# Two halves' filter products issued together, in alternating row groups of TensorE

## The reference

```
emb = radial_embedding(edge_length)              # [E, 8]
h   = silu(emb @ mlp_w0 + mlp_b0)                # [E, 64]
h   = silu(h @ mlp_w1 + mlp_b1)                  # [E, 64]
w   = (h @ mlp_w2 + mlp_b2).reshape(E, 4, 32)    # the filter of an edge
ss, vv = xs[senders], xv[senders]                # gathered rows of a node table
m0 = w[:, 0] * ss
m1 = w[:, 1] * ss * Y1                           # Y1: direction of the edge
m2 = w[:, 2] * vv
m3 = w[:, 3] * (vv . Y1)
msg = segment_sum([m0, m3, m1, m2], receivers)   # [N, 256], then a small product and layer norm
```

## Time and profile before

| | |
|---|---|
| timed runs | 2207.32, 2209.00, 2209.87 us |
| profiled execution | 2202.79 us, span 2201.0 us |
| PE busy | 1899.1 us, 86% of the span |
| PE weight loads | 1431.4 us, 65% |
| DVE busy | 1370.4 us, 62% |
| ACT busy | 637.9 us, 29% |
| POOL busy | 1569.6 us, 71% |
| layer 0 gathers | from 44 to 1048 us |
| layer 1 gathers | from 1133 to 2150 us |
| finish | from 2158 us to the end |

### The profile page before, as it was taken

How to read it: one execution, slowest core, us unless ns; L and a number is a source line. 1 busy time by engine, 2 the same in 40 slices (tenths; PEclk the granted TensorE clock), 3 DMA queues, 4 the chain that set the end, 5 groups by cost and what they waited for, 6 DMA issues and landing times.

```text
span 2201.0 us, 34359 instructions
## 1 busy us (share of the span) xinstructions
PE 1899.1 (86%) x10138; PEld 1431.4 (65%) x10138; DVE 1370.4 (62%) x2905; ACT 637.9 (29%) x995; POOL 1569.6 (71%) x1599
## 2 busy tenths in 40 slices
PE   5887877778777887777879999999999999899997
PEld 4665666666666666666557777666776676677766
DVE  6755555555555555555645776666667666666665
ACT  3643343343433433432541111111111111111114
POOL 4777777777777777777147777777777777777770
PEclk8777777777777777777867998898999998988889
DMA  7422222222222222222021111111121221111112
GB/s 217 126 78 78 76 81 76 76 81 76 76 81 76 80 76 76 81 76 62 6 82 51 55 54 53 53 54 54 53 55 54 54 55 54 52 55 54 53 52 66
DMA packets 105683, 152.31 MB, mean 69 GB/s; under 512 B 33982, under 2 KB 65490, under 8 KB 105546
## 3 DMA queue, kind: packets, MB, share of 16 engines
q0 software_dynamic: 50656, 103.11, 17.3%
q1 hardware_dynamic: 54652, 46.76, 7.0%
q10 hardware_dynamic: 336, 2.01, 0.3%
HBM read 138.53 MB, written 13.21 MB: 69 GB/s over the span
## 4 chain that ended last, share of the span: by engine, by line
POOL 68%; issue 22%; PE 7%; DMA 1%; DVE 1%; ACT 1%; SPq 0%; POOLq 0%; DVEq 0%; ACTq 0%
POOL sent L436 68%; DMA unit_in<-in_x 1%; PE bank L984 1%; PE bank L800 1%; PE bank L767 1%; PE bank L815 1%; PE bank L953 1%; PE bank L759 1%; PE bank L988 0%; PE bank L942 0%; PE bank L871 0%; PE bank L879 0%; PE bank L802 0%; DMA sent<-up_table,senders 0%; DMA sent<-h_table,senders 0%
## 5 line engine op out<-in xcount | busy, mean ns | idle before, releaser
L436 POOL DMA_INDIRECT sent<-up_table,senders x784 | 775.3, 989 | 268.2 <-issue 237.7
L436 POOL DMA_INDIRECT sent<-h_table,senders x784 | 766.5, 978 | 263.9 <-issue 238.6
L815 PE MATMUL bank<-onehot,msg 128*128 128x128 f32 x4704 | 794.0, 332 | 7.1 <-DVE sums L1098 4.2
L815 PEld LDWEIGHTS bank<-onehot,msg 128*128 128x128 f32 x4704 | 706.4, 235 | 116.0 <-issue 91.4
L800 PE MATMUL bank<-Wf_sb,hid 128*128 128x128 f32 x1568 | 281.1, 334 | 94.8 <-DVE hid L1114 94.5
L1124 DVE TENSOR_TENSOR msg<-bank,sent 128x512 f32<-128x512 f32 x196 | 135.6, 692 | 349.1 <-issue 189.7
L800 PEld LDWEIGHTS bank<-Wf_sb,hid 128*128 128x128 f32 x1568 | 246.0, 239 | 153.5 <-DVE hid L1114 100.2
L800 PEld LDWEIGHTS bank<-w_sb,h 64*128 64x128 f32 x1568 | 195.5, 193 | 213.1 <-issue 116.2
L631 ACT ACTIVATE soft<-soft 128x512 f32<-128x512 f32 (+1 forms) x209 | 131.2, 628 | 591.2 <-DVE soft L1105 558.4
L1085 DVE TENSOR_TENSOR onehot<-relT,iota 128x512 f32<-128x512 f32 x392 | 268.8, 686 | 39.3 <-PE bank L815 37.1
L800 PE MATMUL bank<-w_sb,h 64*128 64x128 f32 x1568 | 233.9, 291 | 47.3 <-DVE msg L1157 46.4
(11 more groups left out here) (133 smaller groups left out, 1330.4 us busy)
## 6 DMA issues: line engine op xcount, KB each, us to landing
basis<-in_edge_weight SPq DMA_DIRECT2D x196, 100.0 KB
sent<-h_table,senders POOLq DMA_INDIRECT x784
sent<-up_table,senders POOLq DMA_INDIRECT x784, 2.5
basis<-near_lengths SPq DMA_DIRECT2D x196, 16.0 KB
radial_embedding<-basis SPq DMA_DIRECT2D x196, 16.0 KB
emb_in<-radial_embedding SPq DMA_DIRECT2D x98, 32.0 KB
unit_in<-in_x SPq DMA_DIRECT2D x12, 256.0 KB, 3.7
h_table<-h SPq DMA_DIRECT2D x12, 256.0 KB, 2.8
```

What stands on the lines that cost most here:

```text
L436: pool.indirect_dma_start(sent[:, n % SLOTS, j, :], None, table, bass.IndirectOffsetOnAxis(pick, 0))\
L815: last = t_.matmul(ps[:, k, :], msg[:, p, j, k * P:(k + 1) * P], onehot[:, p, j, :], start=(j == 0), stop=(j == HALF_CHUNKS - 1))
```

## The change

Layer 1's filters get four banks (2, 3, 6, 7: one per slot) in place of two. `filter1` now does both halves of a pair at once: for each of the four chunks it issues the product of the first half (rows 0 to 63 of `h2` and `w2_sb`) and then that of the second (rows 64 to 127), each into its own half's bank, and then the two bias products. So that the second half's bias product also lies in rows from 64 on, `ones_bf` and `bias3` get a second copy of their three rows at row 64, which takes three more small DMAs on SP. `filter1` is called at odd steps only, with the pair h-3 and h-2, where it was called at each step with half h-3. It waits for the messages of half h-6 (four halves before the pair's second) in place of half h-5.

```diff
-    ones_bf = sb("ones_bf", [3, P], BF16)
+    ones_bf = sb("ones_bf", [HIDDEN + 3, P], BF16)
...
-    bias3 = sb("bias3", [3, 3, P], BF16)
+    bias3 = sb("bias3", [HIDDEN + 3, 3, P], BF16)
...
+    filt1 = [quads[i] for i in (2, 3, 6, 7)]
...
         for part in range(3):
-            sp.dma_start(bias3[part:part + 1, :, :], bparts[:, part, :])\
-                .then_inc(d_bparts, 16)
+            for first in (0, HIDDEN):
+                sp.dma_start(bias3[first + part:first + part + 1, :, :], bparts[:, part, :])\
+                    .then_inc(d_bparts, 16)
...
         def filter1(h):
-            p, g = h.parity, h.pair_slot
-            b = h.before(2)
+            o = after(h, 1)
+            g = h.pair_slot
+            b = o.before(SLOTS)
             wait(pe, L1["msg"], b.upto())
             wait(pe, L1["act2"], h.pair_upto())
-            rows = slice(p * HIDDEN, (p + 1) * HIDDEN)
-            products(filtB[p], HALF_CHUNKS, P, lambda j: h2[rows, g, j * P:(j + 1) * P],
-                     w2_sb[rows, :], 2).then_inc(L1["filt"], 1)
+            for j in range(HALF_CHUNKS):
+                for q in (h, o):
+                    rows = slice(q.parity * HIDDEN, (q.parity + 1) * HIDDEN)
+                    t_.matmul(filt1[q.slot][:, j, :], h2[rows, g, j * P:(j + 1) * P],
+                              w2_sb[rows, :], start=(j == 0), stop=False, skip_group_check=True)
+            for q in (h, o):
+                three = slice(q.parity * HIDDEN, q.parity * HIDDEN + 3)
+                t_.matmul(filt1[q.slot], ones_bf[three, :],
+                          bias3[three, 2:3, :].broadcast_to([3, HALF_CHUNKS, P]),
+                          start=False, stop=True, skip_group_check=True).then_inc(L1["filt"], 1)
...
             b = h.before(3)
-            if b.real():
+            if b.parity == 0 and b.real():
                 filter1(b)
...
-        pe.wait_ge(d_bparts, 48)
+        pe.wait_ge(d_bparts, 96)
...
-            filt = filtB[p].rearrange("p j (i m) -> p j i m", m=MUL)
+            filt = filt1[h.slot].rearrange("p j (i m) -> p j i m", m=MUL)
```

More of the change, by code:

```diff
@@ L801, in products @@
                           skip_group_check=True)
-            return t_.matmul(out_bank[0:rows, 0:n_tiles, :], ones_bf[:, 0:rows],
-                             bias3[:, which:which + 1, :].broadcast_to([3, n_tiles, P]),
+            return t_.matmul(out_bank[0:rows, 0:n_tiles, :], ones_bf[0:3, 0:rows],
+                             bias3[0:3, which:which + 1, :].broadcast_to([3, n_tiles, P]),
                              start=False, stop=True, skip_group_check=True)
@@ L923, in layer1_any @@
                 second1(h)
-            filter1(h)
+                filter1(h)
             every_window(L1, every[1], h, 2)
```

## The result

The changed kernel takes 2210.9 us (median of 20 runs, 2206.2 to 2216.3), the kernel before on the same chip 2207.2 (20 runs, 2198.3 to 2212.7). The ratio is 1.0023, with a 95% interval of 1.0014 to 1.0032: slower by about 0.2%, or 3.7 us between the medians, where 7.5 were forecast. The profiled execution took 2212.1 us with a span of 2210.3, against 2202.8 and 2201.0 before: 9.3 us.

A forecast was written before the change was run, and what follows sets the result against it. Layer 1 was taken to be bound by POOL's gathers and the pauses between them. The terms -2 (stall), +5.5 (waits), +4 (end) and 0 (DMAs) made +7.5 on 2209.0: 2216.5 us, 8-in-10 range 2201 to 2226.

The forecast's parts named there:

- What bounds the kernel: Layer 1: POOL's gathers and the pauses between them set the time; PE is off the path except for 4 us.
- The Trainium skill's inference: Layer 1's gathers: by the skill comparisons hold none back, term 0, 2211 us; given 2 in 100 within the no-change case.
- PE's work: Layer 1's filter products: a pair takes 1.52 us instead of 3.10, none of the saving on the path.
- The stall at the start: Start of layer 1: POOL's 3.5 us standstill shrinks as messages come earlier; gain 1 to 3.5 us, taken as 2.
- The wait that goes: Layer 1: DVE's 47.2 us of waits for PE before `add_window` mostly go, moving its comparison; +5.5 us, bounds -7.8 and +11.0.
- the first pattern: Layer 1 iterations where DVE waits for rows only and two comparisons fall on gathers' starts: 20.93 us each, mean 20.69.
- The end: Last window and `finish`: PE at half clock costs +1.7 for the window and +2.6 for one block; taken as +4.
- SP's DMAs: Start of layer 0: three more small DMAs push back its first loads; bounds 0 and 2.5 us, taken as 0.
- The sum: Whole kernel: -2 + 5.5 + 4 + 0 = +7.5 us, on the profiled execution and the timed runs alike.
- it shortens the gathers: Rival, layer 1: small waits for PE settle in the second pattern, 20.52 us an iteration; 2203 us, chance 0.20.
- PE never became the bound: Rival, layer 1: PE stays at half clock over several pairs, each then costing 4 us; 2250 us, chance 0.03.
- Nothing comes of it: Rival, whole kernel: patterns mix as before, the stall's gain and the end's loss nearly cancel; +2, 2211 us, chance 0.27.

The follow-up runs named there:

- the last two kernels with the numbers in PSUM: The changed kernel with layer 1's comparison reading its column numbers from PSUM, 2169.7 us; the same with layer 0's comparison made of four scalar instructions, 2144.8 us.
- two paddings: The changed kernel with one DVE instruction added in layer 1 that nobody reads: a product of 0.28 us, 2193.0 us; or a small sum, 2204.9 us.

## Why the prediction was right, and where not

*What bounds the kernel* held. POOL waits for no message at all in the kernel after, the gathers' length sets the layer, and moving one operand of a comparison is worth 31 us in the kernel before, where four banks without the pairing of PE's products cost as much as the whole change.

*The Trainium skill's inference* ("SBUF — State Buffer", Who interferes with whom), that a product of two SBUF tensors doesn't hold up the writing of descriptors, doesn't carry over to these gathers. In the traces 95 of 95 were held with both operands in SBUF, none of 57 with one in PSUM, nor of the 41 and 48 in the last two kernels with the numbers in PSUM. The same section of the Trainium skill says that a DVE instruction with at most one SBUF input, outside its modes with two ports, doesn't contend with GpSimd; these counts agree. That the gather reads its list of senders in SBUF, and is held by the section's rule for instructions that read there, is argued and was not tried: no run here tells apart which part of a gather is held. The prediction's statement that the term would be nothing by the Trainium skill goes by the inference alone.

*PE's work*: 1.16 us for 16 products and 0.39 for the two biases, 1.13 and 0.39 as taken. Off the path, as said.

*The stall at the start*: forecast -2, measured -3.5: POOL waits for no message any more. The size is within the bounds, the reason only in part the one given. A pair's filters took 2.08 us at half clock, as taken, but for the first pair alone; then the clock was at its upper level, in a stretch where it had been at the lower one. The kernel before and the kernel after (columns as in the earlier trace rows), and PE in the kernel after:

```profile
1147.00:1168.00 21.00, 21.00 (x66) 14.04 (x65) 8.83 (x22) 2.06 (x3) 15.94 (x17) 0.50 0.20 57
```

```profile
1147.00:1184.00 37.00, 32.33 (x238) 22.57 (x236) 29.06 (x69) 6.88 (x10) 28.77 (x28) 1.00 0.20 55
```

```profile
1142.05 2.08 PE L881 MATMUL bank<-h,w_sb 128*128 128x512 f32 x2 [0.78 <-ACT h L696]
1144.05 2.08 PE L893 MATMUL bank<-w_sb,h 64*128 64x128 f32 x16
1146.07 0.58 PE L897 MATMUL bank<-bias,ones_bf 3*128 3x512 bf16 x2
```

The prediction had no term for a clock that rises some 20 us sooner, and why it did isn't shown. That the term came out is thus partly luck. POOL's wait is also gone in the kernel without the alternation, and not in the one with the banks alone; so it goes with both halves in one call, and the overlap isn't needed for it.

*The wait that goes*: forecast +5.5, half of the iterations in the first pattern; measured 45.2 - 34.4 = +10.8, that is nearly all of them, close to the upper bound of +11.0. What was mis-sized is the term against it, that PE falls behind by some 4 us in stretches at half clock. Its prices held: 2.08 us for a pair's filters, 2.08 for a dense product and 0.58 for the biases in the rows above, 3.79 for a window below. But the clock did not stay low for a pair. Between 1147 and 2158 us no 10.4 us, the time of two halves' gathers, has a granted clock under 0.67, that of this stretch:

```profile
1607.00:1617.40 10.40, 9.42 (x53) 7.45 (x54) 7.33 (x18) 0.69 (x1) 7.96 (x9) 0.67 0.22 60
```

PE is busy 9.4 of the 10.4 us there and isn't late, where the prediction had 14.4 us of work. Its window that ran at half clock, in the timelines of PE and DVE:

```profile
1607.98 3.79 PE L817 MATMUL bank<-onehot,msg 128*128 128x128 f32 x16 [1.88 <-DVE msg L1167]
1611.56 1.91 PE L881 MATMUL bank<-h,w_sb 128*128 128x512 f32 x2
1613.40 1.49 PE L893 MATMUL bank<-w_sb,h 64*128 64x128 f32 x16
1614.82 0.39 PE L897 MATMUL bank<-bias,ones_bf 3*128 3x512 bf16 x2
```

```profile
1607.84 0.41 DVE L1108 TENSOR_TENSOR sums<-sums,bank 128x256 f32 x1
...
1612.83 0.41 DVE L1108 TENSOR_TENSOR sums<-sums,bank 128x256 f32 x1
```

That window ended at 1611.77, a microsecond before DVE's next `add_window`, which started without a wait for PE, and PE came back to full clock in the course of the 16 products (1.49 us for 1.16; the biases take 0.39 again). DVE was not delayed, and so the pattern was not lost.

*The end*: forecast +4, measured +1.9 against the first profile. The last window at half clock came (+1.74); the block of `finish` at half clock did not, its products of L998 took 1.02 us from the first on. And the first profile was a lucky one here: against the other two of the kernel before, whose last window ran partly at half clock, the whole end is -0.8 and +0.2 us. So no cost of the change at the end is shown.

*SP's DMAs*: nothing of them is left at layer 1's start (first gather at 1133.02, before at 1132.98).

*The sum*: 7.3 for the gathers and their pauses and 1.9 for the end make the profiled pair's 9.3, against 7.5 forecast; against the two other profiles of the kernel before it is 9.9 and 6.7. The terms came out on both sides of the forecast (-1.5, +5.3 and -2.1 us off), so the nearness of their sum is partly luck. Between the medians it is 3.7, by the step "the sum holds for them alike", which is not shown to hold. The higher executions of the kernel before may have more iterations in the first pattern already, so that less is left to add; its three profiles, all below the median, don't show it, and this stays open. The measured 2210.9 us is thus below the forecast's own range of 2212 to 2224. Of the 5.6 us to 2216.5, 3.8 come from the difference and 1.8 from the median that it was added to, 2209.0 of three runs, for 2207.2 of twenty.

*Readings and sums in it*: the 67 comparisons ended 0.25 to 0.65 us after a gather's start, not 0.3 to 0.6, and 108 ended later than 0.7, not 106, none of them over a held gather. The rival's -11 for an end that costs nothing is -9.8 by its own terms (-7.8 and -2).

Of the rivals, "it shortens the gathers" failed on the waits, which went and did not settle; PE never became the bound. "Nothing comes of it" has the time, 2211 us, by chance: the holds grew by 10.8 us.

## What to carry to other kernels

Where one engine's rhythm sets the time, work taken off another engine can cost: look at what the freed engine will start, and whether that lands on the bound one. Before tuning PE under a gather loop, count the DVE instructions with two SBUF operands that are under way when a gather starts, and give them one operand in PSUM or a scalar form. Do not aim a phase by padding: of two paddings one brought 18 us, with a margin of 0.04 us, and the other ran where the engine would have idled and shifted the comparison by 0.03 us.

## What was not expected of the hardware

The edge is sharp. Over the comparisons of two SBUF tensors in all profiles and both layers, one that starts less than 0.027 us ahead of a gather never holds it, and is itself prolonged (0.75 for 0.68 us at a lead of 0.02); one that starts 0.05 us ahead holds the gather for 0.5 us, one at 0.14 us for 0.4; from 0.027 to 0.045 either happens. A 0.28 us product of DVE that nobody reads made the kernel some 18 us faster. And layer 0's gathers, 975 to 981 ns in every other profile, were no floor of the transfers: with scalar comparisons they take 949.
